# Causal attention with the value products of an item split into two halves of two heads, placed behind the second and the fourth unit of scores

## The reference, cut to what matters

```python
x = x + _L0_attn_ref(_layernorm(x), ...)      # retention
x = x + _L0_ffn_ref(_layernorm(x), ...)       # six layers of local attention and feed forward
x = x + _L1_attn_ref(_layernorm(x), ...)      # causal attention: here
x = x + _L1_ffn_ref(_layernorm(x), ...)       # experts

# _L1_attn_ref: q, k, v [2, 16, 2048, 8]
scores = q @ k.T / sqrt(8); scores = where(kpos <= qpos, scores, min)
out = softmax(scores) @ v;  return out_heads_joined @ Wo.T
```

## Time and profile before

| | us |
|---|---|
| median of 3 runs | 5667.62 |
| lowest to highest | 5661.05 to 5679.34 |
| the profiled execution, its own time | 5660.95 |
| its span | 5659.2 |
| of it, TensorE busy | 5125.1 |
| VectorE, ScalarE, GpSimd busy | 3870.2, 2710.5, 2765.6 |

### The profile page before, as it was taken

The page is one execution under the profiler, slowest core; times in us unless marked ns, Lnnn a source line. Parts: engine busy times, 40 slices in busy tenths (PEclk is TensorE's granted clock), DMA queues, the critical chain, the costliest instruction groups (busy, mean ns, idle before and its releaser), DMA issues.

```text
span 5659.2 us, 159986 instructions
## 1 busy us (share of the span) xinstructions
PE 5125.1 (91%) x71200; PEld 3078.3 (54%) x71200; DVE 3870.2 (68%) x4279; ACT 2710.5 (48%) x3489; POOL 2765.6 (49%) x1297
## 2 busy tenths in 40 slices
PE   8899889998999889988999889986899999998999
PEld 5566646664666556664666456653222222256776
DVE  5988469974889389856898398943666666723333
ACT  1565436653566346643565355642355555541111
POOL 2888458863888278844887198831111111110000
PEclk8999899998999899989999899988799999979999
DMA  1111101111111111110111111102111011000000
GB/s 53 31 37 36 54 18 38 39 35 37 37 36 40 42 28 37 38 58 12 39 37 38 40 32 35 40 21 60 20 18 18 18 27 25 2 34 2 4 4 6
DMA packets 95344, 173.49 MB, mean 31 GB/s; under 512 B 24793, under 2 KB 36706, under 8 KB 93026
## 3 DMA queue, kind: packets, MB, share of 16 engines
q1 hardware_dynamic: 91810, 154.23, 9.7%
q10 hardware_dynamic: 2880, 9.44, 1.2%
HBM read 55.71 MB, written 8.39 MB: 11 GB/s over the span
## 4 chain that ended last, share of the span: by engine, by line
PE 76%; ACT 8%; DVE 6%; issue 4%; POOL 3%; SPq 1%; DMA 1%; ACTq 0%; DVEq 0%; POOLq 0%
PE D L1171 7%; PE D L1090 6%; PE D L1105 5%; PE D L1112 5%; PE D L1022 5%; PE D L1365 4%; PE D L1287 4%; PE D L1129 4%; PE D L1070 4%; PE D L1138 3%; PE D L1140 3%; PE D L1078 3%; ACT V L673 3%; PE D L1250 3%; PE D L1270 3%
## 5 line engine op out<-in xcount | busy, mean ns | idle before, releaser
L448 POOL TENSOR_TENSOR rn<-ss,mhalf 128x32 f32<-128x32 f32 x192 | 1212.2, 6313 | 312.5 <-DVE ss L787 310.4
L897 DVE TENSOR_REDUCE mxp<-D 128x2 f32<-128x1024 f32 (+3 forms) x640 | 672.2, 1064 | 309.5 <-PE D L1254 153.8
L673 ACT ACTIVATE V<-D 128x1024 f32<-128x1024 f32 (+3 forms) x426 | 365.9, 896 | 281.4 <-PE D L1270 280.3
L457 POOL TENSOR_TENSOR XC<-XC,TOK 128x1024 f32<-128x1024 f32 x132 | 311.7, 2361 | 334.8 <-DVE TOK L845 334.6
L845 DVE TENSOR_TENSOR TOK<-D,RA 128x1024 f32<-128x1024 f32 x384 | 466.3, 1214 | 0.0
L453 POOL TENSOR_TENSOR hh<-hh,rr 128x1024 f32<-128x1024 f32 x192 | 364.6, 1899 | 207.8 <-DVE rr L815 207.6
L1171 PE MATMUL D<-PTb,V 64*64 64x32 f32 x24576 | 417.6, 222 | 53.5 <-issue 34.9
L1171 PEld LDWEIGHTS D<-PTb,V 64*64 64x64 f32 x24576 | 398.7, 138 | 95.8 <-issue 95.4
L608 ACT ACTIVATE V<-D 128x512 f32<-128x512 f32 x384 | 229.3, 597 | 445.1 <-PE D L1138 379.9
L785 DVE TENSOR_REDUCE ss<-TOK 128x32 f32<-128x2048 f32 x192 | 436.9, 2276 | 1.1 <-POOL rn L448 1.1
L1105 PE MATMUL D<-RB,XN 128*128 128x512 f32 x768 | 373.2, 609 | 40.2 <-DVE TOK L845 39.3
(11 more groups left out here) (215 smaller groups left out, 10161.9 us busy)
## 6 DMA issues: line engine op xcount, KB each, us to landing
V<-V SPq DMA_DIRECT2D x936, 64.0 KB
V<-V SPq DMA_DIRECT2D x192, 192.0 KB
RA<-tabs_dram SPq DMA_DIRECT2D x6, 2048.0 KB, 7.7
RB<-watt_dram SPq DMA_DIRECT2D x6, 2048.0 KB, 12.1
parts_dram<-hh SPq DMA_DIRECT2D x48, 128.0 KB, 2.3
RA<-parts_dram SPq DMA_DIRECT2D x12, 384.0 KB
TOK<-parts_dram ACTq DMA_DIRECT2D x36, 128.0 KB
RB<-parts_dram SPq DMA_DIRECT2D x12, 384.0 KB
```

What stands on the lines that cost most here:

```text
L448: pool.tensor_tensor(rn[:, st % 2, :], ss[:, :], mhalf[:, :], ALU.pow).then_inc(s["powed"], 1)
L673: act.activation(PTE[i % 3][:, 2 * hp:2 * hp + 2, 0:CH - r * P], pair_of(("S", i + LAG, hp))[:, :].rearrange("p (h n) -> p h n", h=2)[:, : ...
L897: dve.tensor_reduce(mxp[:, 2 * hp:2 * hp + 2, qt, kc], pair_of(("F", at, hp))[:, :].rearrange("p (h n) -> p h n", h=2)[:, :, 0:keys], AX.X ...
```

## The change

`second_values` gets a half hp: it issues the value products of two heads, 2 hp and 2 hp + 1, and waits for the exponential of that half only (`exp2` at 2 i + hp + 1). The first half stands between F1 and S1, the second half where V was. On the diagonal both halves wait for the mask, which waits for both exponentials. `pv2` is raised by the second half alone. Products, operands, banks and results are the same.

```diff
-            def second_values(i):
+            def second_values(i, hp):
 
                 g, n = divmod(i, ITEMS)
                 c, kt = ITEM[n]
                 r = max(0, kt - 4 * c)
-                pe.wait_ge(s["exp2"], 2 * i + 2)
+                pe.wait_ge(s["exp2"], 2 * i + hp + 1)
                 if kt >= 4 * c:
                     pe.wait_ge(s["masked"], diagonals(i))
                 if n == 0:
                     pe.wait_ge(s["vgroup"], g + 1)
                 if kt == 0 and g * CB + c:
                     pe.wait_ge(s["o_copied"], g * CB + c)
-                for h in range(GH):
+                for h in range(2 * hp, 2 * hp + 2):
                     m = pe.matmul(PB[4][32 * h:32 * h + 9, r * P:CH], VG[g % 2][:, h, kt, :], PTE[i % 3][:, h, 0:CH - r * P],
                                   start=(kt == 0), stop=(kt == 4 * c + 3), skip_group_check=True)
-                m.then_inc(s["pv2"], 1)
+                if hp == 1:
+                    m.then_inc(s["pv2"], 1)
...
                     second_scores(i, 0)
                 if at < TOTAL:
                     first_pass(at, 1)
+                if 1 <= i <= TOTAL:
+                    second_values(i - 1, 0)
                 if 0 <= i < TOTAL:
                     second_scores(i, 1)
                 if at < TOTAL:
                     first_pass(at, 0)
                 if 1 <= i <= TOTAL:
-                    second_values(i - 1)
+                    second_values(i - 1, 1)
```

## The result

The changed kernel takes 5800.5 us (median of 4 runs, 5794.4 to 5801.7) against 5666.5 before (median of 4, 5661.1 to 5679.3): 1.0231 times as long, 95% interval 1.0212 to 1.0250. That is slower by 134 us. The direction and most of the mechanism were forecast, the size was not: 5735 us, range 5688 to 5788.

What follows compares the result with a forecast made beforehand. The prediction put the chain of waits first, with PE the fullest engine and a stall in each full item. Its terms, +60 +27 -6 -23 +13 = +71 us on 5660.95, gave 5732, put at 5735 us; range 5688 to 5788.

Steps and rivals of the forecast that it cites:

- The stall and what replaces it: In a full item, PE's 0.46 us stall ahead of the second first-pass unit goes; a half's 0.96 takes its place.
- A half streams as long as the whole: Value products on PE: two heads stream for the same 0.86 us as four, so a half takes 0.96.
- Rival (d): Value products: heads share PE's time, a half takes 0.49 us; some -130 us, 5540 us; chance 0.04.
- rival (c): Value products: the 0.12 us around a half is hidden by its neighbours; -60 us, 5675 us; chance 0.07.
- A full item, 3.68: PE's period with both passes grows from 3.29 to 3.68 us, +0.39; over 177 iterations, weighted by width, +60 us.
- rival (b): Each half pays another 0.10 us for the switch between narrow and whole-array products; +60 us, 5793 us; chance 0.07.
- The rule on draining: Changing the tiling mode drains the engine; the 0.11 to 0.13 us around each value group would be that, already charged.
- Ends of a chunk, +0.9 each: Four iterations at each chunk end, 10.20 us before, take 10.9 and about 0.2 of waits; 30 times, +27 us.
- The waits for the maxima, -23: Seven PE waits for the maxima's transfers shrink from 3.9 us each to 0.5, the clock staying up; -23 us.
- Rival (a): The clock falls at the seven waits for the maxima all the same; +94 us, 5758 us; chance 0.20.
- The last 22 iterations, +13: Without a first pass, PE becomes the bound at 2.80 us an item, up from 1.95; with the eighth wait, +13 us.
- The sum: Whole kernel: 60 + 27 - 6 - 23 + 13 = +71 us on the profiled 5660.95, 5732 us.

Runs made afterwards that it cites:

- e4: Changed kernel, but with one head's value products in the first half and three heads' in the second: 5801.5 us, a single run.
- e5: Changed kernel, but with the value products in four groups of one head, one behind each of the four units: 6355.0 us, a single run.
- e6: Changed kernel with the first half replaced by one full-width fp32 product on the same probabilities: 1.0165 times the kernel before.
- e7: Kernel before the change, with 24 iterations between the passes in place of 22: 5636.2 us, ratio 0.9933.
- e9: Changed kernel split by queries: four heads in both places, 256 columns each in full-width items, first part alone starting the sum, 22 iterations between passes: 5791 us, ratio 1.0252.
- e3: As e9, split by queries with 22 iterations between the passes, but with the start flag on both parts: 5750 us, ratio 1.0119.
- e8: As e9, split by queries with the first part alone starting the sum, but 24 iterations between the passes: 5607.8 us, ratio 0.9874.

## Why the prediction was wrong

By its own steps:

- **The stall and what replaces it.** Right for the full items: F0's wait for the exponential is gone, PE is the bound, and no wait took its place. "Nothing else becomes late" isn't right for the six places where ACT issues transfers: there PE waits longer than before, and twice the clock falls.
- **A half streams as long as the whole.** Right, to the hundredth: 0.96 taken, 0.96 measured, and e4 and e5 show the same for one head and for three. Rival (d), PE's time shared by the heads, is refuted by them, and rival (c), the price around a group hidden, by the 0.96 behind and the 0.53 ahead of every half in the trace after.
- **A full item, 3.68.** This step failed: measured 3.86. The term is the distance from a first-pass unit to the group behind it. I read 0.54 in the earlier trace rows as 0.44 of the unit and 0.10 of a weight load laid bare by the stall, and so let the 0.10 go with the stall. A weight load does stand bare there, but the stall isn't what bares it: it is 0.09 of going into the narrow form, paid ahead of every group. Two groups an item make 0.19, some 297 iterations 56 us. The trace of before had it in plain sight. From a first-pass unit of full width to the values behind it are 0.535 us in the median where that unit had stalled, and the same 0.535 where it had not (133 and 38 places with both passes, at the upper clock). It shows too in the item of the earlier trace rows, where nothing stalls ahead of the values:

```profile
5001.15 0.55 PEld L1270 LDWEIGHTS D<-RB,XC 75*128 75x128 bf16 x4 [0.86 <-ACT V L673]
...
5002.12 0.12 PEld L1287 LDWEIGHTS D<-V,PTb 128*9 128x9 f32 x8 [0.42 <-ACT V L673]
```

  Four instructions of 0.21 are 0.86, and the values start 0.97 behind: 0.11 with no stall to explain it. This is rival (b), "another 0.10 for the switch between narrow and whole-array products", 5793, which I had given 0.07. My argument against it, that the switch was in the 0.97 already, holds for the way out only. The runs don't settle whether the way in is the bare load or a pause of the array.
- **The rule on draining.** The Trainium skill, TensorEngine Tiling (Array Packing), Key Properties, says that a change of the tiling mode drains the engine. The trace agrees in that the weight loads on both sides of a group are not brought forward, and e6 gives the price here, 0.19 us for the way in and out. I cited the rule and counted it once a group, behind it, where it acts on both sides.
- **Ends of a chunk, +0.9 each.** Too small by the same term. The end of the earlier trace rows, 10.20 us, takes 11.70 after (S0 to S0, 4589.91 to 4601.61): +1.5. My sum for it, 10.9 and 0.2 of waits, left out the way into all eight groups, 0.7. The ends of a second chunk grow by 1.4. The six with ACT's transfers in them, at the end of a first chunk, grow by 2.0 to 4.6, 18.9 together. PE waits for the mask five times in the whole layer, once for 0.4 us and four times as here:

```profile
PE D L1287 <- POOL V L495: 2.1, 4, 0.7
```

- **The waits for the maxima, -23.** Right in kind and size. In seven of them 0.49 to 0.86 us of the weight loads' waiting are left, about the 0.5 expected, and PE itself has idle time in only one of these, 0.36 us; behind the one at 4395.22, the partner of the earlier trace rows, the clock stays at its upper level:

```profile
4395.00:4402.00 7.00, 7.00 (x43) 2.28 (x40) 4.08 (x6) 4.58 (x5) 0.59 (x1) 1.00 0.01 3
```

  The time at 1.2 GHz, without the stretch in which the layer starts, falls from 72 to 17 us, and those 17 are the two falls behind ACT's transfers. e7 measured the term alone, 34 us for eight. Rival (a) didn't come.
- **The last 22 iterations, +13.** Right by two errors that cancel. The item takes 3.00 and not 2.80, again the way in twice:

```profile
5142.12 0.60 PE L1270 MATMUL D<-RB,XC 75*128 75x512 bf16 x2
...
5143.62 0.61 PE L1270 MATMUL D<-RB,XC 75*128 75x512 bf16 x2
```

  5143.62 - 5142.12 = 1.50 for a unit and a group. Against that, the clock kept its upper level there.
- **The sum.** +71, with 56 for the way in and 4 more for the last iterations, is +131; 138 are measured in the third layer of the two profiles and 134 between the medians. The rest, some 7, is about what the six ends with ACT's transfers grew beyond the others: 18.9 us against six times 1.4 to 1.7, some 8 to 10 (an estimate). The prediction had no term for them. Smaller errors lie beside these: the 22 items with a first-pass unit of 128 columns take 3.52 where 3.22 was expected, 0.1 more than the two ways in explain.
- **The range** was said to have the half's price as its width, "0.02 on it is 12 us". By that rule its upper end, 53 us above the forecast, stands for 0.09 on each half, which is just the way in. That left no room for anything else to be late, and the result lies 12.5 us beyond it.

## What to carry to other kernels

Narrow products that run side by side in the array are one block of time: a part of the heads costs as much as all of them (0.96 to 0.97 for one to four heads), so dividing such a group by heads doubles its time, while dividing it by columns doesn't (0.56 for half the columns). Each group also pays a way in and a way out. When a duration is read off next to a stall, look for the same pair of operations in a place without one before the excess is put down to the stall. A stage that sits in a ring of three buffers has to be asked which gap limits it, not which engine: one group covered three of four, two half-size groups covered all. And when work is moved, look at each engine's other duties at that place too: ACT's transfers held up an exponential before the change and held it up longer after it.

## What the runs showed of the hardware

- Going from products of full width to products with 9 weight columns and back costs 0.09 us ahead and 0.10 behind at the upper clock, with one head in the group as with more (e4, e5, e6); fp32 after bf16 at full width costs nothing (e6: 0.44 from unit to product).
- Before the change the granted clock fell to 1.2 GHz behind each of seven pauses of 1.5 to 1.8 us; in e6 it didn't behind seven of 0.5 to 0.8. A single pause doesn't tell it alone: in the trace after, it fell behind 1.19 and 1.54 us and not behind one of 2.14 (4612.75) and one of 1.29 (4755.37).
- The reverse was not expected: PE without any gap can stay at 1.2 GHz for 95 us and more (e9, e3), and items with groups of 256 columns let it last (58 us in e8 against 10 in e7 behind like pauses). e8's runs are spread over 53 us, where e7's lie within 19. The Trainium skill, TensorE: Matmul & The Clock Gate, Part 1, has it that "activity releases the throttle"; here busy time alone didn't, and the measurement decides.
- A product with the start flag on some columns of a bank affected sums in the other columns of its rows: e3 and e9 differ in nothing else, and only e3 loses a share of its sum. By the Trainium skill, PSUM — Partial Sum Buffer, The four PSUM rules, the flag clears hidden bits over the whole bank in the 32-row quadrants that the product writes, not over the written columns alone; this pair agrees with it.
